# Splitting GpSimd's subtraction and product of the top-k attention by token tile, in a decoder of six blocks on one core

## The reference

```python
H = 16; d = hid // H; k_keep = int(s * (1.0 - SPARSITY))        # 16 heads of 16, 25 of 256 kept
scores = jnp.einsum('bhqd,bhkd->bhqk', Q, K) / np.sqrt(d)
vals, idx = jax.lax.top_k(scores, k_keep)
sparse = jnp.zeros((n, s)).at[rows, idx].set(vals)               # the others are 0, not -inf
attn = jax.nn.softmax(sparse, axis=-1)
out = jnp.einsum('bhqk,bhkd->bhqd', attn, V)
```

## Time and profile before

| | |
|---|---|
| median of 3 runs | 6089.8 us (6071.2 to 6093.05) |
| profiled execution, span from first to last instruction | 6105.9 us |
| mean granted clock of TensorE | 0.929 |
| TensorE busy | 5431.5 us, 89% |
| VectorE busy | 4571.6 us, 75% |
| ScalarE busy | 3697.2 us, 61% |
| GpSimd busy | 2166.8 us, 35% |

### The profile page before, as it was taken

The page is one execution under the profiler, slowest core; times in us unless marked ns, Lnnn a source line. Parts: engine busy times, 40 slices in busy tenths (PEclk is TensorE's granted clock), DMA queues, the critical chain, the costliest instruction groups (busy, mean ns, idle before and its releaser), DMA issues. The chain is left out here.

```text
span 6105.9 us, 112143 instructions
## 1 busy us (share of the span) xinstructions
PE 5431.5 (89%) x39450; PEld 3840.7 (63%) x39450; DVE 4571.6 (75%) x16189; ACT 3697.2 (61%) x9249; POOL 2166.8 (35%) x3076
## 2 busy tenths in 40 slices
PE   7899998889898899889988898988898889898987
PEld 4666666666666666666666666666666666666654
DVE  2477887777886777887776887777887777887784
ACT  3465666656666655666665666656666556666642
POOL 0233443333343333433333433333433333433331
PEclk7799999999998999999999999999999999998976
DMA  2000000000000000000000000000000000000000
GB/s 87 4 5 6 8 8 6 7 6 6 8 6 8 6 6 6 6 10 8 5 6 8 6 8 7 6 7 6 8 8 6 7 6 6 8 6 6 5 5 6
DMA packets 29372, 53.32 MB, mean 9 GB/s; under 512 B 8145, under 2 KB 9810, under 8 KB 27986
## 3 DMA queue, kind: packets, MB, share of 16 engines
q1 hardware_dynamic: 28770, 45.73, 2.4%
HBM read 37.33 MB, written 8.39 MB: 7 GB/s over the span
## 5 line engine op out<-in xcount | busy, mean ns | idle before, releaser
L1044 DVE MATCH_REPLACE8 wk<-m,wk 128x256 f32<-128x256 f32 x2048 | 820.8, 408 | 0.0
L1065 POOL TENSOR_SCALAR mx<-m 128x2 f32<-128x2 f32 x512 | 120.9, 236 | 1933.8 <-DVE wk L1044 1931.5
L479 DVE TENSOR_REDUCE m_nm<-bankM 128x2 f32<-128x512 f32 x1024 | 650.9, 680 | 158.9 <-PE bankM L469 156.7
L1040 DVE MAX8 m<-wk 128x8 f32<-128x256 f32 x2048 | 758.2, 411 | 0.0
L1074 POOL TENSOR_TENSOR t_pr<-t_pr,sc 128x512 f32<-128x512 f32 x512 | 651.9, 1273 | 40.2
L810 ACT ACTIVATE xk_area<-bankH,xb 64x256 f32<-64x256 f32 x1024 | 479.7, 468 | 297.1 <-PE bankH L712 278.5
L1072 POOL TENSOR_TENSOR t_pr<-wk,sc 128x512 f32<-128x512 f32 x512 | 658.4, 1286 | 2.1 <-PE bankT L570 0.9
L1001 ACT ACTIVATE t_pr<-t_pr,t_nm 128x256 f32<-128x256 f32 x1024 | 464.6, 507 | 212.4 <-POOL t_pr L1074 212.0
L528 PE MATMUL bankM<-m_q,m_kT 32*128 32x512 f32 x2048 | 567.6, 634 | 0.0
L469 PE MATMUL bankM<-m_kT,m_q 32*128 32x256 f32 x4096 | 532.5, 398 | 9.8 <-DVE m_nm L479 8.7
L570 PE MATMUL bankT<-ident,t_pr 128*128 128x128 f32 x2048 | 346.1, 294 | 146.3 <-ACT t_pr L1001 144.0
(11 more groups left out here) (223 smaller groups left out, 11963.2 us busy)
## 6 DMA issues: line engine op xcount, KB each, us to landing
xin<-x_in SPq DMA_DIRECT2D x32, 256.0 KB, 2.6
ctxA<-ctx_in SPq DMA_DIRECT2D x32, 256.0 KB, 2.6
ctxB<-ctx_in SPq DMA_DIRECT2D x32, 256.0 KB, 2.7
out<-x SPq DMA_DIRECT2D x32, 256.0 KB, 2.0
w<-w_w SPq DMA_DIRECT2D x2, 1024.0 KB
xwq<-w_xwq SPq DMA_DIRECT2D x1, 1024.0 KB
xwk<-w_xwk SPq DMA_DIRECT2D x1, 1024.0 KB
xwv<-w_xwv SPq DMA_DIRECT2D x1, 1024.0 KB
```

The source lines that it names most:

```text
L479: nc.vector.tensor_reduce(b["nm"][:, i % 2, 2 * (i // 2) + x, :], banks[u % 4][:].rearrange("p (j s) -> p j s", j=2), AX.X, ALU.max, negat ...
L1040: link.inc(nc.vector.max(top, src[:, t, :]))
L1044: m = nc.vector.match_replace(out=wk[:, k, t, :], in_to_replace=take, in_values=src[:, t, :], imm_value=-BIG)
```

## The change

GpSimd's small maximum waits for the first token tile's top-k alone. The subtraction and the product are made for each token tile in an instruction of its own, in the order subtract 0, subtract 1, multiply 0, multiply 1, and each increments its semaphore. VectorE increments `sp_top` after the last match_replace of either tile (and its own chain semaphore once less). The exponential of a token tile waits for the product of that tile. All other targets are scaled to the doubled counts, and GpSimd executes two instructions more for each head.

```diff
-              dveH=2, dveT=240, ...
+              dveH=2, dveT=224, ...
-              ... sp_mul=16, sp_nm=16, sp_sc=16, sp_tk=16, sp_top=16,
+              ... sp_mul=32, sp_nm=16, sp_sc=16, sp_tk=32, sp_top=32,
@@ raw
                 if u >= 3:
-                    act.wait_ge(*at(g["sp_mul"], u - 2))
+                    act.wait_ge(*at(g["sp_mul"], NT * (u - 2)))
@@ scalar_t
-                act.wait_ge(*at(g["sp_mul"], u + 1))
                 act.wait_ge(*at(g["spa_nm"], u + 1))
                 for t in range(NT):
+                    act.wait_ge(*at(g["sp_mul"], NT * u + t + 1))
                     nc.scalar.activation(b["pr"][:, u % 2, t, :], sp_[:, u % 2, t, :], ACT.Exp,
@@ vector_t
                 if u >= 2:
-                    dve.wait_ge(*at(g["sp_tk"], u - 1))
+                    dve.wait_ge(*at(g["sp_tk"], NT * (u - 1)))
                     dve.wait_ge(*at(g["sp_nm"], u - 1))
...
-                        if r == ROUNDS - 1 and t == NT - 1:
+                        if r == ROUNDS - 1:
                             m.then_inc(g["sp_top"], 1)
@@ pool_t
-                pool.wait_ge(*at(g["sp_top"], u + 1))
+                pool.wait_ge(*at(g["sp_top"], NT * u + 1))
                 nc.gpsimd.tensor_scalar(mx0[:, u, :], m8[:, u % 2, 0, :, 0], 0.0, -1.0, ALU.max, ALU.mult).then_inc(g["sp_nm"], 1)
...
-                nc.gpsimd.tensor_tensor(taken[:, u % 2], wk[:, u % 2], sc[:, u % 3], ALU.subtract).then_inc(g["sp_tk"], 1)
-                pool.wait_ge(*at(g["sp_tk"], u + 1))
-                nc.gpsimd.tensor_tensor(sp_[:, u % 2], taken[:, u % 2], sc[:, u % 3], ALU.mult).then_inc(g["sp_mul"], 1)
+                for t in range(NT):
+                    pool.wait_ge(*at(g["sp_top"], NT * u + t + 1))
+                    nc.gpsimd.tensor_tensor(taken[:, u % 2, t, :], wk[:, u % 2, t, :], sc[:, u % 3, t, :], ALU.subtract).then_inc(g["sp_tk"], 1)
+                for t in range(NT):
+                    pool.wait_ge(*at(g["sp_tk"], NT * u + t + 1))
+                    nc.gpsimd.tensor_tensor(sp_[:, u % 2, t, :], taken[:, u % 2, t, :], sc[:, u % 3, t, :], ALU.mult).then_inc(g["sp_mul"], 1)
```

More of the change, by code:

```diff
@@ L152 @@
               crs_qT=2, crs_rd=2, crs_s=16, crs_sp=4, crs_st=16, crs_v=1, crs_va=1, crs_x=1, crs_y=1, ctxA_in=16, ctxB_in=16, dveC=1,
-              dveH=2, dveT=240, hm_ev=48, hm_ex=32, hm_nm=8, hm_o=8, hm_ot=8, hm_pn=8, hm_proj=12, hm_pt=8, hm_rr=8, hm_s=8, hm_tr=8,
+              dveH=2, dveT=224, hm_ev=48, hm_ex=32, hm_nm=8, hm_o=8, hm_ot=8, hm_pn=8, hm_proj=12, hm_pt=8, hm_rr=8, hm_s=8, hm_tr=8,
               hm_vev=4, hm_vtr=4, hm_x2=1, hm_xb=1, hm_y=1, latT=1, lat_ps=1, len_in=16, lin_o=1, lin_xb=1, lin_y=1, ln0_rstd=1, ln0_stat=5,
@@ L159 @@
               mla_m3=1, mla_m3p=1, mla_nm=16, mla_on=2, mla_onT=1, mla_ont=1, mla_ot=2, mla_ott=1, mla_pv=8, mla_q=1, mla_qT=2, mla_rd=2,
-              mla_s=16, mla_sp=4, mla_st=16, mla_v=1, mla_va=1, mla_x=1, mla_y=1, sp_mul=16, sp_nm=16, sp_sc=16, sp_tk=16, sp_top=16,
+              mla_s=16, mla_sp=4, mla_st=16, mla_v=1, mla_va=1, mla_x=1, mla_y=1, sp_mul=32, sp_nm=16, sp_sc=16, sp_tk=32, sp_top=32,
               sp_xb=1, spa_ex=32, spa_k=1, spa_kT=2, spa_nm=16, spa_on=2, spa_onT=1, spa_ont=1, spa_ot=8, spa_ott=1, spa_pt=16, spa_pv=8,
```

## The result

The changed kernel runs in 6019.24 us (median of 4 runs, 6008.8 to 6033.22), the kernel before beside it in 6091.43 us (6071.2 to 6102.36): the ratio is 0.9886 with a 95% interval of 0.986 to 0.9911. The forecast was 6074 us with a range of 6048 to 6102. The profiled execution of the kernel after has a span of 6031.4 us, against 6105.9 before.

A forecast was written before the change was run, and what follows sets the result against it. The prediction took the latency chain VectorE, GpSimd, ScalarE, TensorE to decide in about one head in five. 15.4 us before the drain plus 0.8 in it, together 16 us, off the 6089.8 us median gave 6074 us, range 6048 to 6102.

The forecast's parts named there:

- the latency step: At heads where VectorE, GpSimd, ScalarE, TensorE wait in chain, the exponentials' end comes 0.59 us sooner after the last match_replace.
- The price of a half: A GpSimd subtraction or product at 128x256 takes 740 ns, between bounds of 0.64 and 1.05 us.
- the back-to-back gaps: GpSimd's four halves each start 0.04 us before the predecessor's record ends, together 2.84 us against 2.62 now.
- the moments at a tight head: After the last match_replace: first subtraction at 0.13 us, last product's end at 2.97, second exponential's end at 3.50.
- ScalarE's and TensorE's waits at the exponentials: ScalarE's total wait for GpSimd's product falls from 212 to about 160 us, TensorE's for the exponentials from 144 to 120.
- VectorE's wait for the layernorm rows: VectorE's waits for layernorm rows, 18.7 us for the largest group, rise by a few us.
- lies beside other work except where a late operation stands behind it: GpSimd's 0.22 us more a head, 113 us over 512 heads, costs only where a late operation is queued behind.
- The gain is larger: Rival, chance 0.18: the gain also works through other queues, giving 6029 us by ScalarE's waits or 6050 by TensorE's clock.
- the first, all of ScalarE's waits: Way to the larger gain: all 103 ScalarE waits for the product cut by 0.59 us each, 61 us, giving 6029 us.
- The second, the clock: Way to the larger gain: eight low-clock stretches of TensorE after waits for the exponentials saved, 24 us more, giving 6050 us.
- "Nothing": Rival, chance 0.14: VectorE is the late engine, TensorE meets its next result at the same time; within 5 us of 6090.
- "Slower": Rival, chance 0.10: GpSimd's halves cost more than their share; gain gone at 0.82 us a half, 6135 us at 1.05.

The follow-up runs named there:

- e1: The changed kernel's split of subtraction and product by token tile, but every wait as in the kernel before; ratio to before 0.9856, 6004.67 us.
- e3: The kernel before, all waits kept, with subtraction and product in halves at head 15 of each sequence only; ratio to before 0.989, 6028.68 us.
- e4: The changed kernel with whole-width subtraction and product at head 15 alone; ratio to the kernel before 0.9927, 6053.51 us.
- e7: Split by token tile with the waits of the kernel before, and pieces of 128 columns at head 15; ratio to before 0.9841, 6011.07 us.
- e9: The kernel before with eight idle matmuls in front of TensorE's wait for VectorE's L907; ratio to before 0.9917, 6052.03 us.
- e8: The changed kernel's instructions and waits run once more; ratio to the kernel before 0.9882.
- e12: The changed kernel with head 15's operations in quarters and its start as before; ratio to the kernel before 0.9799, 5970.16 us.

## Why the prediction was wrong

**Right.** The sign, though mostly for another reason: e1 gains as much without the latency step, and this part is luck. The price of a half (740 ns worked out, 741 and 732 measured), the back-to-back gaps, the moments at a tight head (to 0.04 us), ScalarE's and TensorE's waits at the exponentials (160 and 120 us forecast, 141.5 and 117.7 measured), and that the first exponential's early start gives TensorE nothing by itself. The early start alone gained 9 us at equal clock where its share of the sum is 11 (0.40 of 0.59 of 16). A few us more were forecast for VectorE's wait for the layernorm rows; it didn't grow (18.7 us before, 18.6 after).

**Wrong, first: the sum lacked a term.** The step that failed is the sentence that GpSimd's longer work "lies beside other work except where a late operation stands behind it". I looked for who waits for GpSimd by a semaphore and in its queue. The trace of before showed a third way, a shorter GpSimd operation that frees VectorE sooner: VectorE's L907 had 271 ns at the least and 1270 as its median, the duration of a GpSimd operation to 3 ns. The sum put this term at nothing. Neither the list of waits nor the chain of waits shows this, since it is not idle time but a longer busy time. By e3 and e1 it is 32 to 37 us at equal clock, from 512 columns to 256, and in the change's 50 it is 24 to 26 by e4 and the 12 us of TensorE's wait for lnM_xn; by e7 another 30 to 128 columns.

**Wrong, second: the size of the clock.** The forecast gave the clock nothing in its sum and 24 us more in a rival, by way of TensorE's wait for the exponentials; it left VectorE out as an engine "which the change doesn't touch". The change does touch VectorE's L907, which TensorE waits for at L768. The clock's part was 18 to 26 us for the change and 54 for the split alone; e9 shows that such a gain comes from this one wait with nothing else changed. The forecast also said that a mean clock that moves by 0.01 would outweigh all else; it moved by 0.005, worth 26 us.

**The rivals.** "The gain is larger" came true. Of its two ways, the first, all of ScalarE's waits, didn't: those waits fell by 70 us, but TensorE's for the exponentials by 26. The second, the clock, came near its 24 us, through another wait than it named. The port term was in neither. "Nothing" describes the latency alone rather well: in e4 18 of the 23 us that TensorE saved at the exponentials came back at its wait for VectorE, the sign that the forecast had named for this rival. "Slower" didn't come; the point from which it would turn, a half of 0.82 us, was not reached. That the split alone is as fast as the whole change in all was in no case of mine, and it turns the forecast round: the part I costed as a loss (0.22 us later where another operation stands behind it) is the part that pays most, and the part I costed as the gain is worth 0 to some 10 us at equal clock on top of it (e8 against e1, e12 against e7), which these runs can't tell from nothing once the clock has its say.

## What to carry to other kernels

Compare the minimum and the median duration of the same operation on VectorE: a fixed-shape operation whose median is several times its minimum is held up by something, and if the median equals the duration of a GpSimd operation, shorten that one, first of all where VectorE's operation is what TensorE waits for. Splitting a GpSimd operation costs it 15% here, and it needs to be done only for the one head in sixteen that runs beside the sensitive place. Where TensorE's longest recurring wait is, look at the granted clock just behind it: the wait and the slow stretch are one item of the account. And when one of TensorE's waits gets shorter, see whether the next one got longer by as much.

## What the runs showed of the hardware

- VectorE's tensor_scalar and two-input operations lasted as long as the GpSimd operation beside them: 1270, 734 to 758 and 465 ns for GpSimd operations of 512, 256 and 128 columns, with 271 ns undisturbed. Their ends follow the GpSimd operation's end by a fixed time (0.28 us for L902, to 3 ns). None of its 8192 max8 and match_replace lasted over 0.43 us before.
- GpSimd's own operations lengthened too beside such VectorE operations: a subtraction took 1.51 us at 2027.54 in place of 1.27, and a small maximum 0.39 in place of 0.22.
- Eight idle matmuls in front of one recurring wait of 4.2 us made a kernel 0.8% faster with all else unchanged (interval of the ratio 0.9892 to 0.9941).
- Runs of one kernel beside each other spread by 33 to 42 us, and 5.0 us for each thousandth of mean granted clock explain this to 3.6 us.
